# Another order for the first 74 microseconds of a decoder layer: products of zeros between TensorE's jobs, the keys' high rows first, weights later, values ahead of the context, one row by a second queue

## The reference

```python
x = x + attn(layernorm(x))       # softmax(q @ k.T / 4 - slope_h * |i - j|) @ v, then @ out_w.T
x = x + xattn(layernorm(x), ctx) # one head of 256: softmax(q @ k.T / 16) @ v
x = x + ffn(layernorm(x))        # top 2 of 8 experts: relu(x @ W1[e] + b1[e]) @ W2[e] + b2[e]
```

## Time and profile before

| | us |
|---|---|
| median of 3 executions (lowest to highest) | 1512.07 (1510.06 to 1518.13) |
| the profiled execution: its time, its span | 1522.94, 1521.1 |
| TensorE busy in that span | 1480.3 (97%) |
| DVE, ACT, POOL busy | 1156.9 (76%), 1021.0 (67%), 417.6 (27%) |

### The profile page before, as it was taken

How to read it: one execution, slowest core, us unless ns; L and a number is a source line. 1 busy time by engine, 2 the same in 40 slices (tenths; PEclk the granted TensorE clock), 3 DMA queues, 4 the chain that set the end, 5 groups by cost and what they waited for, 6 DMA issues and landing times.

```text
span 1521.1 us, 28830 instructions
## 1 busy us (share of the span) xinstructions
PE 1480.3 (97%) x9696; PEld 892.5 (59%) x9696; DVE 1156.9 (76%) x2550; ACT 1021.0 (67%) x1840; POOL 417.6 (27%) x459
## 2 busy tenths in 40 slices
PE   8999999999999999999999999999999899999997
PEld 4524443344444434445444344337999899999996
DVE  7889887888888788888877878745788787665563
ACT  3266667667656676755666765788777688776673
POOL 5002010012110042300004110043446665454453
PEclk8999999999999899999999999999999999999998
DMA  5644053023050431304144030053667988899993
GB/s 130 131 67 77 30 125 43 10 34 43 29 125 30 70 64 36 43 33 94 33 67 85 16 43 29 28 196 94 174 183 226 259 235 226 250 267 259 256 266 80
DMA packets 82018, 170.64 MB, mean 112 GB/s; under 512 B 14699, under 2 KB 48735, under 8 KB 79183
## 3 DMA queue, kind: packets, MB, share of 16 engines
q1 hardware_dynamic: 66447, 143.17, 37.3%
q0 software_dynamic: 15424, 25.63, 8.3%
HBM read 130.86 MB, written 34.36 MB: 109 GB/s over the span
## 4 chain that ended last, share of the span: by engine, by line
PE 86%; DVE 5%; ACT 3%; issue 2%; SPq 1%; DMA 1%; POOL 0%; POOLq 0%; ACTq 0%; DVEq 0%
PE ps L1333 16%; PE ps L1306 15%; PE ps L1292 13%; PE ps L1561 4%; PE ps L1542 4%; PE ps L1562 4%; PE ps L1563 4%; PE ps L1540 4%; PE ps L1541 3%; PE ps L1439 2%; PE ps L1405 2%; ACT prob L1580 2%; PE ps L1295 2%; DVE sums L1763 2%; PE ps L1544 2%
## 5 line engine op out<-in xcount | busy, mean ns | idle before, releaser
L1580 ACT ACTIVATE prob<-ps 128x512 f32<-128x512 f32 x1024 | 562.5, 607 | 292.7 <-PE ps L1292 159.8
L1333 PE MATMUL ps<-stacked_k,stacked_q 112*128 112x512 bf16 x1024 | 391.2, 388 | 8.6 <-DVE rmax L1763 3.3
L1763 DVE CUSTOM_DVE_ANT_0 sums<-ps,ramps 128x512 bf16<-128x512 f32 x480 | 328.5, 684 | 85.8 <-PE ps L1333 79.1
L1765 DVE TENSOR_REDUCE rmax<-ps 128x1 f32<-128x512 f32 x480 | 326.7, 686 | 73.4 <-PE ps L1333 68.8
L1292 PE MATMUL ps<-stacked_q,stacked_k 115*128 115x512 bf16 x1024 | 362.8, 383 | 3.9 <-ACT prob L1580 1.8
L1333 PEld LDWEIGHTS ps<-stacked_k,stacked_q 112*128 112x128 bf16 x1024 | 99.9, 99 | 314.8 <-DVE rmax L1763 113.7
L1306 PE MATMUL ps<-prob,values 128*32 128x512 f32 x2048 | 274.5, 608 | 1.1 <-issue 0.6
L2203 POOL DMA_INDIRECT out<-yo,token_of x71 | 141.2, 1988 | 189.4 <-DVE yo L2087 144.1
L1713 ACT ACTIVATE hid<-ps,w_now 128x256 f32<-128x256 f32 (+1 forms) x312 | 124.2, 451 | 86.8 <-PE ps L1542 62.2
L1292 PEld LDWEIGHTS ps<-stacked_q,stacked_k 115*128 115x128 bf16 x1024 | 99.6, 98 | 103.4 <-ACT prob L1580 55.8
L1561 PE MATMUL ps<-w_high,hid_high 128*128 128x256 f32 x512 | 149.5, 292 | 1.4 <-DVE sums L2081 1.4
(11 more groups left out here) (246 smaller groups left out, 2400.8 us busy)
## 6 DMA issues: line engine op xcount, KB each, us to landing
w_now<-in_w SPq DMA_DIRECT2D x78, 514.0 KB
w_now<-in_w SPq DMA_DIRECT2D x78, 512.0 KB
stacked_q<-parts_of_rows SPq DMA_DIRECT2D x84, 128.0 KB, 7.1
stacked_k<-parts_of_rows SPq DMA_DIRECT2D x84, 128.0 KB, 7.7
xi<-expert_rows SPq DMA_DIRECT2D x71, 130.0 KB, 2.9
parts_of_rows<-q_part SPq DMA_DIRECT2D x21, 256.0 KB, 2.8
...
```

The lines of the kernel that those rows point to most:

```text
L1333: m = e.matmul(ps[:, bank, :], qa[i][0:MAX_ROW, hh, qt * P:(qt + 1) * P], ka[i][0:MAX_ROW, hh, kc * BANK:(kc + 1) * BANK], start=True, sto ...
L1580: e.activation(prob[:, u % NPROB, :], ps[:, score_bank(u), :], ACT.Exp, scale=SLOPE ** (k[0] % NG * HG + k[3])).then_inc(sem["exp"], 1)
L1763: e.tensor_tensor_reduce(sums_16[:, :], of, ramp_beside(1 - qt % 2, qt % 4), 1.0, -3.0e38, ALU.add, ALU.max, into).then_inc(sem["maxed"], 1)
L1765: e.tensor_reduce(into, of, AX.X, ALU.max).then_inc(sem["maxed"], 1)
```

## The change

Six edits, all about group 0. (1) Fifteen products of zeros of 128x512 in three places of TensorE's list (6, 5 and 4), and six more between the turns of the second half of the rows, two after each of three. (2) ACT makes the high parts of q and k before it normalizes row tile 4, and `direct` of the keys' high part moves up, ahead of the queries' middle part on the queues. (3) Scaling and splitting the weight pieces 1 and 2, and POOL's `fill` (fixed entries of keys and values), move behind the second half's projections and thus behind the first eight maxima. (4) The planner assumes the context 4 us later and may put a side step where DVE is still at work, which puts the values ahead of the context. (5) `nrow` drops one of five instructions. (6) The third maximum row of group 0 is sent from ACT's queue instead of SP's.

```diff
-CONTEXT_LANDS = 12.0
+CONTEXT_LANDS = 16.0
...
             add("x_low", 0, c, 0)
+        add("warm", 6)
...
         for a in range(2):
             for i in range(p.parts(("proj",))):
                 p.add_part(i, "proj", 0, 0, a, 0)
-            for n, kind in enumerate(("high", "rest", "mid", "low")):
-                if (a, kind) == (0, "rest"):
-                    add("shift", "pre", 0, AFT)
-                    add("norm", "pre", 0, AFT[0])
+            add("high", 0, 0, a, 0)
+            add("direct", a, 0, 0)
+        add("warm", 5)
+        for a in range(2):
+            add("rest", 0, 0, a, 0)
+            if a == 0:
+                add("shift", "pre", 0, AFT)
+            for n, kind in enumerate(("mid", "low"), 1):
                 add(kind, 0, 0, a, 0)
-                if kind != "rest":
-                    add("direct", a, n - (n > 0), 0)
+                add("direct", a, n, 0)
         add("specials")
-        for tt in range(AFT[0] + 1, AFT[1]):
+        for tt in range(*AFT):
             add("norm", "pre", 0, tt)
-        add("fill")
...
         flush()
-        add("scale_q", 1)
-        for i in range(1, DC + 1):
-            add("w_high", i)
-            add("w_low", i)
+        add("warm", 4)
         for a in range(2):
             yield from project(0, 0, a, 1)
             flush()
             for n in range(NPART):
                 add("direct", a, n, 1)
+        add("fill")
+        add("scale_q", 1)
+        for i in range(1, DC + 1):
+            add("w_high", i)
+            add("w_low", i)
         add("context_in")
...
+    def pair_free():
+        place = len(p.rings["max"]) + 1
+        before = p.holder.get(p.max_bank(place // UNITS, place))
+        return 0.0 if before is None else p.emptied.get((EMPTIED[before[0]], *before[1:]), float("inf"))
...
-        elif beside and (p.open or p.room() <= p.pe + 0.3) and (now["maxima"] >= gone or not 0 < now["maxima"] < UNITS or now["context_at"] == float("inf")):
+        elif beside and (p.open or p.room() <= p.pe + 0.3) and (now["maxima"] >= gone or p.pe + 0.6 <= pair_free() or not 0 < now["maxima"] < UNITS or now["context_at"] == float("inf")):
...
+                        if (b, c, four) == (0, 0, 1) and q < 3:
+                            warm(2)
...
+                elif kind == "max_rows" and k == [0]:
+                    e.wait_ge(sem["nrow"], 1)
+                    max_row(e, 0, NPART - 1)
...
-                    then(e.tensor_scalar(nrow[:, :], ps[0:HG * NT, p.bank("max_turn", G), 0:P], -1.0, None, ALU.mult))
-                    e.tensor_copy(nparts[:, 0, :], nrow[:, :]).then_inc(sem["nrow_part"], 1)
+                    maxima = ps[0:HG * NT, p.bank("max_turn", G), 0:P]
+                    e.tensor_scalar(nparts[:, 0, :], maxima, -1.0, None, ALU.mult).then_inc(sem["nrow_part"], 1)
                     e.wait_ge(sem["nrow_part"], 2 * G + 1)
-                    then(e.tensor_tensor(nrest[:, :], nrow[:, :], nparts[:, 0, :], ALU.subtract))
+                    then(e.scalar_tensor_tensor(out=nrest[:, :], in0=maxima, scalar=-1.0, in1=nparts[:, 0, :], op0=ALU.mult, op1=ALU.subtract))
...
-                    e.wait_ge(sem["rstd"], p.upto("rstd", "pre", 0, AFT))
+                    e.wait_ge(sem["low"], p.upto("low", 0, 0, 1, 1))
                     key_ones(2)
```

23 lines of the change are left out of this document (14 added, 9 removed).

## The result

The changed kernel takes 1520.14 us (median of 19 runs, 1515.11 to 1525.38) against 1513.29 for the kernel before on the same chip (19 runs, 1508.6 to 1518.8). The ratio is 1.0047, with a 95% interval of 1.0034 to 1.006: slower by 6.85 us, where 1512.3 and no change were forecast.

A forecast was written before the change was run, and what follows sets the result against it. DVE's reductions were taken to set the pace from 24.77 us, TensorE before that. Terms -3.2 + 3.0 - 3.0 + 3.1 + 0.2 = +0.1, with roundings +0.2, took 1512.07 to 1512.3 us; range 1506 to 1517.

The forecast's parts named there:

- the sum: Shift of the first score from all terms: -3.2 + 3.0 - 3.0 + 3.1 + 0.2 = +0.1 us, with roundings +0.2.
- the landing of the keys' low rows: Before the first maximum: low part done at 17.5, rows landed at 20.8 us, bounds 20.1 and 21.3.
- The method: The change is worth how much earlier the first score starts, from 74.37 us; all that follows moves with it.
- The start: DVE's first reduction of group 0 at 21.6 us, 3.2 earlier, between 2.2 and 3.9.
- My sign for being wrong: First reduction past 22.6 us; also listed: no TensorE hole between maxima 8 and 9, or a changed 1447 us after the score.
- What DVE gets in return: Behind the first reduction DVE gets one more `rest` (0.65) and `scale_q` with both `w_low` (2.4): 3.0 us later.
- The wait that takes its place: TensorE waits 4.5 us for `w_low` ahead of maximum 9; DVE then stalls 1.6 or 3.1 us, 3.1 taken.
- the end of the context's wait: DVE's wait for the context during group 0's reductions goes, as its transfers leave sooner: 3.0 us earlier.
- Reductions end at 21.6 + 36.8 + 3.9 + 2.4 + 3.1 = 67.8: Group 0's last reduction on DVE: start, reductions, six `rest`, weights and stall add to 67.8 us, as before.
- From there to the score: From the last reduction's end N to the first score: N + 6.8 against N + 6.6 before, 0.2 us later.
- The wait for `spread 1`: TensorE, behind `max_turn`, waits 1.5 us for group 1's rows, whose transfers run from N - 16.2 to N + 1.8.
- it loses: Rival, chance 0.2: zeros fail to hold TensorE's clock; first reduction at 23.9, score 2.5 us later at 76.8, time 1514.6.

The follow-up runs named there:

- e2: The changed kernel with the scaled and split weights and the `fill` back in their old, early place; ratio to the kernel before 0.9991.
- e14: A second profile of the changed kernel, unchanged; first reduction at 23.08, `nmax` at 74.66, first score at 82.34 us.
- e13: A second profile of the kernel before, unchanged; first reduction at 25.00, `nmax` at 65.57, first score at 72.15 us.
- e1: The changed kernel without the rule that lets a side step stand between two maxima of a pair; ratio to the kernel before 1.0081.
- e6: The kernel before with the products of zeros alone added; ratio to the kernel before 0.9982, first score at 69.41 us.
- e9 to e12: The kernel before with zeros plus one part each: weights late 1.0016, keys' high rows first 1.0004, steps inside a pair 1.0025, new row of maxima 0.998.
- e3: The changed kernel without any products of zeros; ratio to the kernel before 1.0072, first score at 80.52 us.

## Why the prediction was wrong

Two steps of the sum make most of the error: the landing of the keys' low rows (2.1 us, with the late `x`), and the new rule for pairs, which I put at nothing (4.1 us of waits stand where the sum has none, 3.3 of them for maxima). And the earlier start, which was to pay for the later weights, does not come from them: with the weights back in their old place (e2) the start is as early and the whole loss is gone.

**The method stood.** The first score sets the time: a straight line through the 15 timed kernels rises by 1.0 us of time per us of first score (correlation 0.93), and single kernels lie up to 3.7 us off it. By that line a score 8.85 us later is 8.8 us of time, where 6.85 were measured; with the second profiles of both kernels it would be 10.2.

**The start: predicted 21.6, came 23.70.** Clock 1.00 from 10 to 20 us and the early high parts were right. The step that failed is the landing of the keys' low rows. I took 20.8 for the landing, from a low part done at 17.5 and 2.6 to 3.8 of transfer. The low part was done at 18.1 (`x` came later in this execution; in e14 the first reduction is at 23.08, so 0.6 of the 2.1 us are that), SyncE sent it at 18.29, and the maximum could start at 22.87, 4.5 later, beyond my upper bound. I had read the landings off a median and off a window of DMA traffic. The transfers one by one say it better: in the trace of before the last of the four, issued at 18.80, landed at 22.51, 4.4 behind the low part (18.13). Sent sooner, behind the high rows, the last one took 4.5 instead of 3.7 and landed 4.7 behind the low part: what the earlier issue gave, the transfer took. It is so in each of the ten executions with the high rows first (4.5 to 4.6) and each of the seven without (3.6 to 3.7). The four of the changed kernel:

```profile
stacked_k<-k_part SPq DMA_DIRECT2D x4, 64.0 KB, 4.0
```

My sign for being wrong (first reduction past 22.6) was met. With the weights gone from there, VectorE stood idle for 3.71 us, a hole that I had in no step.

**What DVE gets in return: right in the sum of work (3.0), wrong in what it replaces.** I counted the weights' 2.4 us as work moved behind the first reduction, at its own price, and took the earlier start as the gain from it. But in the old place they fill the wait for the rows: e2, with them there, has its first reduction at the same time as without. Their removal bought nothing.

**The wait that takes its place: right in kind, 4.5 predicted, 5.25 measured.** It ends with `w_low` as I said, and the half level behind it was there. The fifth reduction came 12.8 behind the first instead of 11.5: 0.9 because `w_low` took 1.56 beside GpSimd's subtraction, the rest because the clock was at half for all of what is queued behind. The 3.0 us that the end of the context's wait was to bring were read from an execution with the half level behind that wait; in e13 VectorE lost 0.66 us there.

**The term that was missing: the steps between the maxima of a pair.** "Reductions end at 21.6 + 36.8 + 3.9 + 2.4 + 3.1 = 67.8" lets VectorE run without a wait from the fifth reduction on. It waited 4.1 us from 40 us on, 0.76 of them for ScalarE's high part. I had read the context's wait as gone, which it was, and had given the new rule of `pair_free` no price at all, though it was in the diff: a value's or context's product then stands between two maxima that free one after the other, and with four maxima in PSUM VectorE catches up. TensorE's timeline of the changed kernel, at one such place (the six products between are left out):

```profile
50.17 0.39 PE L1349 MATMUL ps<-stacked_k,stacked_q 112*128 112x512 bf16 x1
50.80 0.39 PE L1349 MATMUL ps<-stacked_k,stacked_q 112*128 112x512 bf16 x1 [0.24 <-DVE rmax L1776]
...
51.74 0.82 PE L1349 MATMUL ps<-stacked_k,stacked_q 112*128 112x512 bf16 x3
```

So `nmax` was 8.1 late: 2.1 of the start, 1.3 of the hole and 4.7 behind it (4.1 of waits, the rest the overlap of neighbours that each wait breaks).

**From there to the score: N + 6.8 predicted, N + 7.3 measured.** The wait for `spread 1` was 0.57 and ended at N + 1.2, against 1.5 and N + 1.8: the transfers began at N - 18.7 (57.15) and not N - 16.2, since VectorE's waits lay between, and their rows were there after 20.0 us and not 18.0. The half level behind it (76.2 to 79.6) cost the rest.

**How the parts add.** On the base with zeros, the weights' place costs 0.0034, the rule for pairs 0.0043, the keys' high rows with the planner's answer 0.0022, the zeros gain 0.0018 and the row of maxima 0.0002. That adds to 0.0079, and the whole is 0.0047: the parts do not simply add, and e1 shows that taking the pair rule away from the whole kernel makes it slower still, with the `yield` edit left in. Two parts were never run alone, that edit and the context time of 16. Each ratio has an interval of about 0.002 and a difference of two about 0.003, and e6 was timed on another chip than e9 to e12, so their order is not settled; that the weights' place is enough for all of the loss is (e2).

My rival "it loses" had the right sign for the wrong reason: it had the zeros fail, and they held the clock and, in e6, brought the first score forward by 2.7 to 5.0 us.

**What stays open.** e3 is slower than the changed kernel by the times (0.0025, inside the intervals) while its profiled first score is earlier; only the clock behind `nmax` was found as a reason. The stretch behind the first score varies by 14 us with the time at the half level; why the clock falls in one execution and not in another of the same order was not shown. Nor was what the `yield` edit costs or gives alone.
